# Windowed attention of a two-layer vision block: weighted values together, projection in the fourth score bank, statistics behind the key copy

## The reference

```python
xn = layernorm(x, norm1_g, norm1_b)                  # over the 96 channels of each token
xs = roll(xn, (-4, -4)); xw = windows_of_8x8(xs)     # 4 windows of 64 tokens an image
q, k, v = split(xw @ qkv_w + qkv_b)                  # 12 heads of 8 channels
attn = softmax(q * SCALE @ k.T + bias[None] + mask)  # 64 x 64 for each window and head
out = (attn @ v) @ proj_w + proj_b
x = shortcut + roll(windows_back(out), (4, 4))       # the residual
# then: x + mlp(layernorm(x)), and the second layer
```

## Time and profile before

| | |
|---|---|
| median of 3 runs | 552.92 us (550.82 to 564.15) |
| the profiled execution | 551.77 us, span on the core 549.8 us |
| granted TensorE clock, mean | 0.972 |
| busy share: PE, PEld, DVE, ACT, POOL | 92%, 61%, 61%, 56%, 32% |
| first and last matmul of a score (L706) | start at 29.4 and 250.5 us of the span |

### The profile page before, as it was taken

One profiled execution on the slowest core, in us unless ns is written; L12 is line 12 of the kernel. 1 busy time (PEld: TensorE's weight loads), 2 busy tenths in 40 slices (PEclk: granted clock), 3 DMA queues, 4 the chain that ended last, 5 costly groups with the idle time before them and its releaser, 6 DMA issues. The chain is left out here.

```text
span 549.8 us, 27773 instructions
## 1 busy us (share of the span) xinstructions
PE 505.5 (92%) x11496; PEld 337.2 (61%) x11496; DVE 337.8 (61%) x875; ACT 310.2 (56%) x763; POOL 176.7 (32%) x217
## 2 busy tenths in 40 slices
PE   7789999999999999999799999939999999999996
PEld 6767667667666666767575433219665565656553
DVE  1158888888888888887602473356456656566544
ACT  1138888888888888886533655302444444444432
POOL 8224444443333344444220202003353323333200
PEclk9779999999999999999999999977999999999998
DMA  3111111111111111100031132322464444434411
GB/s 76 25 49 33 32 31 42 26 26 25 29 29 29 29 29 29 29 4 4 1 82 37 39 88 66 96 61 55 113 167 112 110 121 118 113 105 114 120 50 30
DMA packets 40899, 32.62 MB, mean 59 GB/s; under 512 B 18954, under 2 KB 36491, under 8 KB 40843
## 3 DMA queue, kind: packets, MB, share of 16 engines
q1 hardware_dynamic: 37258, 26.11, 18.8%
q0 software_dynamic: 3584, 5.72, 4.7%
HBM read 18.36 MB, written 7.13 MB: 46 GB/s over the span
## 5 line engine op out<-in xcount | busy, mean ns | idle before, releaser
L391 POOL TENSOR_TENSOR scores<-scores,peak 128x768 f32<-128x768 f32 x64 | 92.9, 1473 | 148.1 <-DVE peak L555 148.1
L1235 POOL DMA_DIRECT2D x_stack<-padded_x x96 | 52.4, 548 | 96.3 <-PE ps_v L1508 59.8
L454 ACT COPY probs_t<-ps_probs 128x768 f32<-128x768 f32 x64 | 51.1, 799 | 18.8 <-PE ps_out L733 9.4
L548 DVE TENSOR_TENSOR scores<-ps_scores,bias 128x1536 f32<-128x1536 f32 x32 | 55.3, 1727 | 6.3 <-PE ps_scores L706 6.2
L716 PE MATMUL ps_probs<-ident,scores 128*128 128x128 f32 x384 | 55.9, 282 | 0.1
L555 DVE TENSOR_REDUCE peak<-scores 128x24 f32<-128x1536 f32 x32 | 55.8, 1744 | 0.1
L448 ACT ACTIVATE scores<-scores 128x768 f32<-128x768 f32 x64 | 54.2, 847 | 0.4 <-POOL scores L391 0.4
L733 PE MATMUL ps_out<-v_blocks,probs_t 128*32 128x18 f32 x3072 | 38.9, 187 | 15.2 <-DVE stream L574 15.1
L733 PEld LDWEIGHTS ps_out<-v_blocks,probs_t 128*32 128x32 f32 x3072 | 32.5, 110 | 31.5 <-issue 17.6
L1048 ACT ACTIVATE hidden<-ps_hidden,fc_b_folded 128x512 f32<-128x512 f32 x48 | 29.1, 688 | 36.5 <-PE ps_hidden L989 36.5
L1508 PE MATMUL ps_qk<-x_stack,conv_w 40*32 40x256 f32 x1536 | 48.8, 379 | 0.0
(11 more groups left out here) (159 smaller groups left out, 907.2 us busy)
## 6 DMA issues: line engine op xcount, KB each, us to landing
x_stack<-padded_x SPq DMA_DIRECT2D x96, 54.0 KB
x_stack<-padded_x POOLq DMA_DIRECT2D x96, 54.0 KB, 2.8
padded_x<-x_pad SPq DMA_DIRECT2D x32, 121.5 KB, 2.7
x_sliced<-stream SPq DMA_DIRECT2D x48, 64.0 KB, 2.0
mixed<-y_sliced SPq DMA_DIRECT2D x48, 64.0 KB, 2.0
out<-y_sb SPq DMA_DIRECT2D x32, 96.0 KB, 2.0
x_now<-in_x SPq DMA_DIRECT2D x32, 72.0 KB, 1.8
stream<-in_x SPq DMA_DIRECT2D x32, 72.0 KB, 1.9
```

The lines of the kernel that those rows point to most:

```text
L391: nc.gpsimd.tensor_tensor(sc, sc, peak[:, par, p, :].unsqueeze(2).to_broadcast((128, HEADS, WN)), ALU.subtract).then_inc(s["shifted"], 1)
L454: nc.scalar.copy(probs_t[:, :], ps_turned).then_inc(s["turned_copied"], 1)
L548: nc.vector.tensor_tensor(scores[:, par, :, :].rearrange("p a (g c) -> p a g c", g=NG), ps_scores[:, :, 0:PAIRS * TRIO * WN].rearrange("p ...
L1235: engine.dma_start(x_stack[64 * half + i * HC:64 * half + (i + 1) * HC, slot, :, :], rows).then_inc(landed[slot], 16)
```

## The change

- `weigh(t+1, 0)` and `weigh(t+1, 1)` stand together at the end of TensorE's step; probs_t holds both pairs.
- ps_proj moves from the bank ps_out to the fourth bank of ps_scores. `score` now waits until the residual of the image two before it is done, and `weigh` no longer waits for a residual. `project` and `make_v` get waits of their own for the last images, where no later part implies them.
- TensorE's `turn_heads(t)` moves ahead of `turn_back` and of `make_q_and_k`, right behind `turn(t+1, 0)`.
- VectorE's `measure` moves to the end of the step, behind `copy_k`, and takes image t+5; `add_residual(t)` stands behind it, where before `add_residual(t-1)` stood near the start of the next step. `add_bias` stays ahead of `weigh_heads`.
- ScalarE's second `exponent` goes ahead of `copy_turned(t+1, 0)`, and `copy_ot` ahead of `copy_q`.
- In the last steps the first statistics of the next stage come behind `weigh_heads`, and the filler matmuls go to another bank.

```diff
-    probs_t = sb("probs_t", [128, SC])
+    probs_t = sb("probs_t", [128, PAIRS, SC])
...
-    ps_proj = ps_out[0:C, 0, N:2 * N]
+    ps_proj = ps_scores[0:C, 3, 0:N]
...
         def copy_turned(t, p):
-            need(act, s["pv_ready"], u)
-            nc.scalar.copy(probs_t[:, :], ps_turned).then_inc(s["turned_copied"], 1)
+            need(act, s["pv_ready"], u - 1)
+            nc.scalar.copy(probs_t[:, p, :], ps_turned).then_inc(s["turned_copied"], 1)
...
             if real(t + 1):
+                exponent(t + 1, 1, 1 - par)
                 copy_turned(t + 1, 0)
...
-            if real(t + 1):
-                exponent(t + 1, 1, 1 - par)
+            if real(t):
+                copy_ot(t, par)
             if real(t + 3):
                 copy_q(t + 3)
-            if real(t):
-                copy_ot(t, par)
...
         def step(t, half, par):          # VectorE
             if real(t + 4):
-                measure(t + 4)
-                await_stats(t + 4)
-            if real(t - 1):
-                add_residual(t - 1, half, par)
-            if real(t + 4):
                 gather_spread()
...
-            if is_image(t, B - 2):
-                measure_tokens(nc, dve, m, s2, 0, by_blocks(first_homes[0]))
             if real(t):
                 weigh_heads(t)
             if is_image(t, B - 2):
+                measure_tokens(nc, dve, m, s2, 0, by_blocks(first_homes[0]))
                 measure_tokens(nc, dve, m, s2, 1, by_blocks(first_homes[1]))
...
             if real(t + 3):
                 copy_k(t + 3)
+            if real(t + 5):
+                measure(t + 5)
+                await_stats(t + 5)
+            if real(t):
+                add_residual(t, half, par)
...
         def make_v(t, par):
+            if past(t + 1):
+                pe.wait_ge(s["biased"], B)
...
             need(pe, s["v_copied"], t * 2)       # in score(t)
+            need(pe, s["residual_done"], t - 2)
...
                 need(pe, s["ot_copied"], t * PAIRS)      # in weigh(t, p)
-            else:
-                need(pe, s["residual_done"], t)
...
         def project(t, par):
             pe.wait_ge(s["ot_copied"], (t + 1) * PAIRS)
+            if past(t + 2):
+                need(pe, s["residual_done"], t)
...
         def step(t, half, par):          # TensorE
-            if real(t):
-                weigh(t, 1, par)
             if real(t + 1):
                 turn(t + 1, 0, 1 - par)
+            if real(t):
+                turn_heads(t)
...
-            if real(t):
-                turn_heads(t)
...
                 turn(t + 1, 1, 1 - par)
-                weigh(t + 1, 0, 1 - par)
             if real(t):
                 project(t, par)
             if real(t + 5):
                 turn_tokens(t + 5, half + 2 + par, 1 - par)
+            if real(t + 1):
+                weigh(t + 1, 0, 1 - par)
+                weigh(t + 1, 1, 1 - par)
```

More of the change, by code:

```diff
@@ L570, in add_residual @@
         def add_residual(t, half, par):
-            dve.wait_ge(stream_in[1 - par], half * 32 if par == 0 else (half + 1) * 32)
+            dve.wait_ge(stream_in[par], (half + 1) * 32)
             dve.wait_ge(s["proj_ready"], t + 1)
@@ L733, in weigh @@
                     mm = nc.tensor.matmul(ps_pv[32 * part:32 * part + 32, p, 2 * q:2 * q + 2, :],
-                                          probs_t[:, at:at + 32], v_blocks[:, par, p, part // 2, q, :, :],
+                                          probs_t[:, p, at:at + 32], v_blocks[:, par, p, part // 2, q, :, :],
                                           start=True, stop=True, skip_group_check=True)
@@ L840, in _ @@
         led_image_loop(pe, step)
-        fill(nc, ps_scores[0:C, 3, 0:C], blank[:, :], 16)
+        fill(nc, ps_out[0:C, 0, 0:C], blank[:, :], 16)
         for c in range(SLICES):
```

## The result

The changed kernel takes 629.16 us (median of 4 runs, 625.95 to 636.09) against 554.5 us for the kernel before on the same chips: a ratio of 1.135 with a 95% interval of 1.125 to 1.146. The ratio leaves out one run on each side that fell in the chip's slower state (636.09 and 564.15). The profiled execution took 629.68 us for a span of 627.8, 77.9 more than that of before. The page's shares and its clock row come first; they answer to the clock in the earlier trace rows.

What follows compares the result with a forecast made beforehand. It took the attention loop's TensorE ring, 7.15 us a step, as the bound. Terms +47.3, +2.2, +0.6 and -1.6 gave +48.5 on 551.8, so 600.3 (601.4 from the median); it said 601 us, range 588 to 626.

Steps and rivals of the forecast that it cites:

- What bounds the kernel: Attention loop: TensorE's block plus its wait for the residual form a ring of 7.15 us a step, VectorE and ScalarE close behind.
- turn_heads waits for a division behind the bias, 3.43 us after the score: TensorE's step: turn_heads starts 3.43 us after the score starts, held by score, bias and division, with only one turn as cover.
- Two waits on one ring, 8.90 us a step: Loop step: waits for division and residual follow one another, so a step takes 8.90 us, 1.75 more, 27 times: +47.3.
- the pitch behind turn_back, 0.56: TensorE's step: time from the start of turn_back to the start of q, 0.56 us, part of the 3.65 behind turn_heads.
- +50.1: Attention stage to its last score: +47.3 for full steps, +2.2 for two later steps, +0.6 at the start.
- The clock stays at 1.00: Attention loop: the granted clock of TensorE doesn't leave 1.00 despite the new idle times, as the forecast of 601 us assumes.
- a rival at 0.26 with 622 us: Attention loop: the new TensorE stall makes the clock fall once in every step, giving 622 us; chance 0.26.
- The rival's price, 22 us: Attention loop: one fall of the clock in each of 27 steps at 0.8 us each, 22 us; chance 0.26.
- The stage's end: -1.6 us: End of attention: 1.0 us of turn_heads' wait and one residual wait of about 0.6 go, -1.6 us.
- The shorter path (589): Before the next score: TensorE's own path, not the residual, is last, score at 8.48 us, +1.33 a step, 589; chance 0.12.
- the faster case (534): At turn_heads: the division is done in time, TensorE runs back to back at 6.5 us a step, -17.6, 534; chance 0.05.

Runs made afterwards that it cites:

- e10: The kernel before with only TensorE's turn_heads(t) moved ahead, right behind turn(t+1, 0): 575.9 us.
- e3_fill8: The changed kernel with 8 filler matmuls, result unused, between turn(t+1, 0) and turn_heads(t) on TensorE for images 0 to 27: 605.9 us.
- e3_fill4: The changed kernel with 4 filler matmuls, result unused, between turn(t+1, 0) and turn_heads(t) on TensorE for images 0 to 27: 604.6 us.
- e1: The changed kernel with VectorE dividing the heads of image t before it adds the bias of image t+2: 574.6 us, ratio to before 1.036.
- e2: The changed kernel with TensorE's turn_heads(t) back behind make_q_and_k(t+3), VectorE still bias first: 590.6 us.
- e5: The changed kernel with the residual before the statistics, copy_q before copy_ot, second weighting behind the score, turn_heads behind q and k: 566.8 us.
- e7: e5 with the one-column VectorE operation behind the statistics reading one operand from PSUM, in place of both from SBUF: 560.6 us.
- e4: e1 with VectorE's residual of image t also ahead of the statistics of image t+5, a one-column operation behind these: 568.4 us.
- e8: e7 with the next stage's two weight foldings ahead of the last image's turn_heads on TensorE: 555.9 us, ratio to before 1.004.
- e11: e8 with both weightings of image t behind the score of image t+2, none at the step's end: 548.45 us, ratio to before 0.984.

## Why the prediction was wrong

The direction and the mechanism of the chain were right, the number was not. Point by point:

- *What bounds the kernel.* Right: the loop's rings on TensorE and VectorE decide in every run.
- *turn_heads waits for a division behind the bias, 3.43 us after the score.* Right: 3.52, and e10 shows that this part alone costs 22 us.
- *Two waits on one ring, 8.90 us a step.* Right in kind, the size a little high: without the fall a step takes 8.6, which is 38.1 us in the 26 steps (e3_fill8) where I had 45.5. The term that was too large is the pitch behind turn_back, 0.56. I read it as TensorE's own, but it was q waiting for the bias, which had ended 0.15 us before it. In the new order the bias is long done, and the pitch is 0.22. Up to the last score I had +50.1 against +45.9, which looks closer than it is: the first and last steps took 7.8 us more, not 4.6, some of it falls of the clock.
- *The clock stays at 1.00.* **This is the step that failed.** I had it as a rival at 0.26 with 622 us. I called the row that spoke for it thin evidence, one idle time of 1.40 in front of one fall. It was the only row shown with an idle time near the new one, and it should have weighed more than the many steps at 0.66. The rival's price, 22 us, came out (22.2 in the 26 steps) by two errors that cancel. I gave each fall 0.8 us, as if it lay anywhere in the step, and one fall to every step. The falls came in 18 of 26 steps, and each cost 1.2 to 1.3, because they begin right behind the stall, where TensorE is the path.
- The Trainium skill (TensorE: Matmul & The Clock Gate, "A second HAM failure mode: psum-queue depth-cycling") has the clock swing between its levels where the engine is often idle for a short time between groups of matmuls. The trace agrees that the clock swings in a loop without waits for transfers, 0.86 in the middle of the stage. That the idle times are frequent and short didn't suffice here: e3_fill4 has 1.1 and 0.5 us in every step at a clock of 1.00.
- *The stage's end: -1.6 us.* Wrong in sign, +6.2. I took waits away one by one and did not ask whether they would join to a single long one, here of 2.69 us. 4.8 of the 6.2 are the clock behind it.
- The shorter path (589) and the faster case (534) didn't occur. The second needs the division first and more besides: e1 removes the wait of turn_heads and is still at 574.6.
- The sum with both: 551.8 + 45.9 + 23.6 + 6.2 = 627.5, and 2.2 of start and later stages to 629.7. The range ended at 626 since it took the stage's end to be 1.6 us shorter even where the clock falls.

## What to carry to other kernels

A part that waits for a long chain belongs behind as much independent work of its own engine as the chain is long; moving it up, or moving the cover away, turns hidden latency into step time. When a change creates an idle time on TensorE that is longer than those the trace has at full clock, look at the idle time in front of each fall of the clock in that same trace and price the fall into the forecast, at the place where it will begin: right behind the new idle time. A gap between two instructions that follow each other with no listed wait can still be a wait; compare its end with the ends on the other engines. Waits that are removed one by one can join into one.

## What was not expected of the hardware

- With an idle time of 1.8 us in each step the clock fell in most steps, 18 of 26, and not in the others. With one of 1.1 us (e3_fill4), or 0.5, 1.1 and 0.35 us in one step (e2), it never did in the loop's middle; with 0.65 and 0.90 us shortly after one another it did in two steps of one execution (e10). So a single long idle time isn't the only way down, and the border isn't known.
- A VectorE operation of one column took 908 ns with both tensor operands in the SBUF, while GpSimd was at work, and 218 ns with one in the PSUM (means of e5 and e7). The Trainium skill (SBUF — State Buffer, "Who interferes with whom") says that an operation with two SBUF inputs contends with GpSimd's reads and one with a single SBUF input doesn't; the runs agree.
- In front of every second score, where no wait covers it, TensorE stands about 0.5 us with nothing shown (e4 to e8). That fits one gap for each turn of the hardware loop, which takes two images and turns 12 times. In the kernel before and in e11 a wait for the residual stands there and the steps are nearly even (7.21 and 7.12, 6.85 and 6.87), so it hides most of it. Its cause wasn't tried.
